# Narrow attentions: a bias row added behind the mix, and fp16 projections in the last attention

## The reference

```
def attention(query, ctx, mask, Wq, bq, Wk, bk, Wv, bv, Wo, bo):   # per batch of 256 tokens
    q = query @ Wq.T + bq;  k = ctx @ Wk.T + bk;  v = ctx @ Wv.T + bv     # 16 heads x 8
    scores = einsum('bhsd,bhtd->bhst', q, k) / sqrt(8)       # layer 1: + bias, mask; layer 3: none
    attn = softmax(scores)
    return einsum('bhst,bhtd->bhsd', attn, v).reshape(B, S, 128) @ Wo.T + bo
x = x + attention(layernorm(x), ctx, ...)
```

## Time and profile before

| | us |
|---|---|
| median of 3 runs | 1505.87 |
| lowest, highest | 1499.92, 1507.51 |
| profiled execution, its own time | 1497.63 |
| span of its instructions | 1495.7 |
| TensorE matmuls busy in it | 1357.8 |
| VectorE, ScalarE, GpSimd busy | 1038.6, 888.9, 820.1 |

### The profile page before, as it was taken

How to read it: one execution, slowest core, us unless ns; L and a number is a source line. 1 busy time by engine, 2 the same in 40 slices (tenths; PEclk the granted TensorE clock), 3 DMA queues, 4 the chain that set the end, 5 groups by cost and what they waited for, 6 DMA issues and landing times.

```text
span 1495.7 us, 37017 instructions
## 1 busy us (share of the span) xinstructions
PE 1357.8 (91%) x14494; PEld 838.4 (56%) x14494; DVE 1038.6 (69%) x2508; ACT 888.9 (59%) x1471; POOL 820.1 (55%) x778
## 2 busy tenths in 40 slices
PE   4799999998979999999978899987978897999988
PEld 3365666665757777777733344433666565444446
DVE  5788888888744344443758989875798476677764
ACT  4487777774759999999834444432233332555542
POOL 6488878776658899989844243212353002434310
PEclk9799999999989999999979999986989899899998
DMA  8000000000013210001101201000000000000000
GB/s 273 5 9 9 9 9 9 2 2 16 30 33 98 61 45 14 28 28 46 33 5 32 65 33 33 30 1 28 1 3 10 0 1 4 5 9 9 2 1 29
DMA packets 25796, 39.62 MB, mean 26 GB/s; under 512 B 7028, under 2 KB 13080, under 8 KB 25144
## 3 DMA queue, kind: packets, MB, share of 16 engines
q1 hardware_dynamic: 25080, 35.58, 7.4%
q0 software_dynamic: 576, 2.10, 0.7%
HBM read 38.72 MB, written 1.05 MB: 27 GB/s over the span
## 4 chain that ended last, share of the span: by engine, by line
PE 67%; DVE 19%; issue 5%; POOL 5%; ACT 3%; DMA 1%; SPq 0%; POOLq 0%; DVEq 0%; ACTq 0%
PE bank L1765 10%; PE bank L1706 10%; PE bank L695 5%; DVE sbuf L834 4%; PE bank L633 4%; PE bank L2231 3%; PE bank L1164 2%; PE bank L649 2%; PE bank L1989 2%; PE bank L1268 2%; POOL sbuf L1118 2%; PE bank L2210 2%; DVE sbuf L851 2%; PE bank L1196 2%; POOL sbuf L1112 2%
## 5 line engine op out<-in xcount | busy, mean ns | idle before, releaser
L1716 ACT ACTIVATE sbuf<-bank,sbuf 128x512 f32<-128x512 f32 (+1 forms) x512 | 323.1, 684 | 30.1 <-PE bank L1706 18.1
L1736 POOL TENSOR_TENSOR sbuf<-sbuf 128x512 f16<-128x512 f32 x256 | 304.9, 1199 | 56.1 <-ACT sbuf L1716 55.1
L310 POOL TENSOR_TENSOR sbuf<-sbuf 128x2 f32<-128x2 f32 (+1 forms) x48 | 39.7, 827 | 353.8 <-DVE sbuf L305 353.8
L1765 PEld LDWEIGHTS bank<-sbuf 128*128 128x128 f16 x3072 | 194.3, 98 | 67.3 <-issue 7.7
L1765 PE MATMUL bank<-sbuf 128*128 128x128 f16 x3072 | 214.6, 220 | 6.3 <-DVEq L1853 6.3
L1706 PE MATMUL bank<-sbuf 128*128 128x512 f16 x768 | 209.2, 382 | 0.0
L834 DVE TENSOR_REDUCE sbuf<-bank 128x4 f32<-128x1024 f32 x128 | 156.3, 1221 | 64.4 <-PE bank L649 51.5
L1848 DVE SCALAR_TENSOR_TENSOR sbuf<-bank,sbuf 128x128 f32<-128x128 f32 x256 | 71.7, 341 | 165.1 <-PE bank L1765 164.9
L1118 POOL TENSOR_TENSOR sbuf<-sbuf 128x512 f16<-128x512 f32 x128 | 148.2, 1179 | 56.8 <-ACT sbuf L1361 56.7
L695 PE MATMUL bank<-sbuf 128*32 128x256 f32 x2048 | 140.3, 393 | 1.6 <-ACT sbuf L782 1.6
L1112 POOL TENSOR_TENSOR sbuf<-sbuf 128x512 f16<-128x512 f32 x96 | 112.0, 1185 | 27.4 <-ACT sbuf L1349 27.1
(11 more groups left out here) (294 smaller groups left out, 2726.8 us busy)
## 6 DMA issues: line engine op xcount, KB each, us to landing
sbuf<-w SPq DMA_DIRECT2D x32, 256.0 KB, 2.9
sbuf<-bias_t SPq DMA_DIRECT2D x4, 1024.0 KB, 11.7
sbuf<-ctx_t SPq DMA_DIRECT2D x24, 128.0 KB, 3.4
sbuf<-bias_q POOLq DMA_DIRECT2D x4, 512.0 KB, 11.6
sbuf<-mask_t SPq DMA_DIRECT2D x8, 256.0 KB, 2.7
sbuf<-bias_t SPq DMA_DIRECT2D x8, 256.0 KB, 3.0
sbuf<-mask_q SPq DMA_DIRECT2D x8, 256.0 KB, 3.7
sbuf<-bias_q SPq DMA_DIRECT2D x8, 256.0 KB, 4.4
```

Source lines behind the costliest of these rows:

```text
L1716: last = act.activation(to, bank[u % 4][:, :], ACT.Gelu, bias=b1[u // U][:, u % FT0:u % FT0 + 1], scale=1 / SCALE)
L1736: g.tensor_tensor(hid16[1][:, u % BUFS, :], hid[:, u % 4, :], hid16[0][:, u % BUFS, :], ALU.subtract)\
L1765: last = pe.matmul(bank[4 + out_no % 2][:, j * P:(j + 1) * P], hid16[h][:, u % BUFS, j * P:(j + 1) * P], w2_16[p][:, w, f * D:(f + 1) * D] ...
```

## The change

It has two parts. In both narrow attentions the bias matmuls of the v and of the output projection go. Once a layer TensorE computes `bv @ Wo.T + bo` (`row` on TensorE, at unit 4), VectorE writes it as three bf16 rows beside a row of ones (`row` on VectorE, at unit 5), and `out` starts each output with three one-row bf16 matmuls over both tiles of 128 tokens, ahead of its wait for the normalised mix. In layer 3 alone the projections of q, k and v become three fp16 passes over halves (high x high, high x low, low x high), with the weights scaled by 256 and ScalarE's scale taking it back. GpSimd makes the halves: of the weights (`weights16`) behind the first `power` of the FFN ahead, of the inputs of batch 0 (`inputs16`) behind the second, and of batch b + 1 behind the splits of batch b.

```diff
-            ("bv1", [D]), ("bo1", [D]),
+            ("bv1", [1]), ("bo1", [D]),
...
+            def weights16(g):
+                at = 0
+                for w, to in zip((wq, wk0, wv), w16):
+                    flat = w if w is wv else w.rearrange("p t c -> p (t c)")
+                    cols = flat.shape[1]
+                    g.tensor_tensor(flat, flat, scale_col[:, 0:1].to_broadcast([P, cols]), ALU.mult)\
+                     .then_inc(s["sixteen"], 1)
+                    g.wait_ge(s["sixteen"], at + 1)
+                    g.tensor_copy(to[:, 0, :], flat).then_inc(s["sixteen"], 1)
+                    g.wait_ge(s["sixteen"], at + 2)
+                    g.tensor_tensor(to[:, 1, :], flat, to[:, 0, :], ALU.subtract).then_inc(s["sixteen"], 1)
+                    at += 3
+
+            def inputs16(g, b):
+                cols = slice(b * S, b * S + S)
+                g.wait_ge(ctx_in[b % 2], b // 2 * 16 + 16)
+                g.wait_ge(nrm_xt, nm.ready(b))
+                wait(g, s["projected"], JOBS * (b - 1))
+                for n, (to, of) in enumerate(((c16[b % 2], ctx_t[b % 2]), (x16[b % 2], xn_t[:, cols]))):
+                    g.tensor_copy(to[:, 0, :], of).then_inc(s["sixteen"], 1)
+                    g.wait_ge(s["sixteen"], WEIGHTS + 4 * b + 2 * n + 1)
+                    g.tensor_tensor(to[:, 1, :], of, to[:, 0, :], ALU.subtract).then_inc(s["sixteen"], 1)
...
                     for k in range(QK):
                         split_(b, k)
+                    if not masked and b + 1 < B:
+                        inputs16(g, b + 1)
...
+                            for n, (w, half16) in enumerate(PASSES):
+                                last = pe.matmul(to[:, c * S:(c + 1) * S], w16[kind][:, w, m * P:(m + 1) * P],
+                                                 (c16 if kind else x16)[b % 2][:, half16, :],
+                                                 start=c == n == 0, stop=c == 1 and n == 2, skip_group_check=True)
...
-                            pe.matmul(o, ct[:, t * P:(t + 1) * P], wv, start=True, stop=False)
-                            last = pe.matmul(o, ones[0:1, :], bv[0:1, :], start=False, stop=True)
+                            if masked:
+                                last = pe.matmul(o, ct[:, t * P:(t + 1) * P], wv, start=True, stop=True)
+                                continue
+                            for n, (w, half16) in enumerate(PASSES):
+                                last = pe.matmul(o, c16[b % 2][:, half16, t * P:(t + 1) * P], w16[2][:, w, :],
+                                                 start=t == n == 0, stop=t == 1 and n == 2, skip_group_check=True)
...
+                def row():
+                    pe.matmul(bank[O_BANK[1]][0:1, 0:D], bv, wo, start=True, stop=False)
+                    pe.matmul(bank[O_BANK[1]][0:1, 0:D], ones[0:1, 0:1], bo[0:1, :], start=False, stop=True)\
+                      .then_inc(s["row"], 1)
...
                 def out(b):
-                    pe.wait_ge(s["normed"], b + 1)
...
+                    if b == 0:
+                        pe.wait_ge(s["row"], 5)
+                    for k in range(3):
+                        pe.matmul(bank[PR][:, 0:S], row16[0:1, 3, :], row16[0:1, k, :].unsqueeze(1).to_broadcast([1, SB, D]),
+                                  start=k == 0, stop=False, skip_group_check=True)
+                    pe.wait_ge(s["normed"], b + 1)
                     for m in range(SB):
-                        o = bank[PR][:, m * P:(m + 1) * P]
-                        pe.matmul(o, att_t[:, m * P:(m + 1) * P], wo, start=True, stop=False)
-                        last = pe.matmul(o, ones[0:1, :], bo[0:1, :], start=False, stop=True)
+                        last = pe.matmul(bank[PR][:, m * P:(m + 1) * P], att_t[:, m * P:(m + 1) * P], wo, start=False,
+                                         stop=m == 1, skip_group_check=True)
...
+                    src, rest = bank[O_BANK[1]][0:1, 0:D], rden[0:1, 0:D]
+                    v.wait_ge(s["row"], 1)
+                    v.tensor_copy(row16[0:1, 0, :], src).then_inc(s["row"], 1)
+                    v.wait_ge(s["row"], 2)
+                    v.tensor_tensor(rest, src, row16[0:1, 0, :], ALU.subtract).then_inc(s["row"], 1)
+                    v.wait_ge(s["row"], 3)
+                    v.tensor_copy(row16[0:1, 1, :], rest).then_inc(s["row"], 1)
+                    v.wait_ge(s["row"], 4)
+                    v.tensor_tensor(row16[0:1, 2, :], rest, row16[0:1, 1, :], ALU.subtract).then_inc(s["row"], 1)
...
                 for k in range(CHUNKS):
                     after.power(g, 2 * k, 2 * k + 2)
+                    if k == 0:
+                        ahead["weights"](g)
+                    if k == 1:
+                        ahead["inputs"](g)
```

More of the change, by code:

```diff
@@ L197, in build @@
             far[name] = take(shape)
+        row_parts = [take([4, D], BF16) for _ in range(2)]
         x_in = [sem(f"x_in{k}") for k in range(CHUNKS)]
@@ L521, in narrow_attention @@
                 "ready",
-            ) if masked or k not in ("masks", "biased")}
+                "row",
+                "sixteen",
+            ) if k not in (("sixteen",) if masked else ("masks", "biased"))}
             ctx_in = [sem(L + f"ctx_in{p}") for p in range(2)]
@@ L540, in narrow_attention @@
             bqs = take([HG])
+            row16 = row_parts[0 if masked else 1]
+            if not masked:
+                w16 = [take([2, HG * P], F16), take([2, HG * P], F16), take([2, D], F16)]
+                x16, c16 = [take([2, S], F16)], [take([2, S], F16)]
+                assert top[0] <= 29888
             if masked:
@@ L559, in narrow_attention @@
             att_t = take([S])
+            if not masked:
+                top[0] = max(top[0], 21040)
+                x16, c16 = x16 + [take([2, S], F16)], c16 + [take([2, S], F16)]
+            SCALE = 1.0 if masked else 2.0 ** 8
+            PASSES = ((0, 0), (0, 1), (1, 0))
+            WEIGHTS = 9
             assert top[0] <= 24832
@@ L632, in project @@
                         for c in range(2):
-                            last = pe.matmul(to[:, c * S:(c + 1) * S], (wq, wk0)[kind][:, 2 * pair + c, :],
-                                             ct if kind else xt, start=True, stop=True)
+                            m = 2 * pair + c
+                            if masked:
+                                last = pe.matmul(to[:, c * S:(c + 1) * S], (wq, wk0)[kind][:, m, :],
+                                                 ct if kind else xt, start=True, stop=True)
+                                continue
[3 more added lines that the diff above has]
+                                                 start=c == n == 0, stop=c == 1 and n == 2, skip_group_check=True)
                     else:
@@ L737, in tensor @@
                         mix(u // 2 - 1, n % 2)
+                    if u == 4:
+                        row()
                     if b + 1 < B and n < JOBS:
@@ L762, in project @@
                             last = act.activation(x32[:, k % 2, c * S:(c + 1) * S], src[:, c * S:(c + 1) * S], ACT.Identity,
-                                                  bias=bias, scale=DH ** -0.5 if kind == 0 else 1.0)
+                                                  bias=bias, scale=(DH ** -0.5 if kind == 0 else 1.0) / SCALE)
                     else:
@@ L910, in narrow_attention @@
             ahead["masks"] = lambda v, k: masks(v, 0, k)
+            ahead["weights"], ahead["inputs"] = weights16, lambda g: inputs16(g, 0)
             programs["sync"].append(sync)
```

21 lines of the change are left out of this document (17 added, 4 removed).

## The result

| | before | after |
|---|---|---|
| median, us | 1504.03 (5 runs) | 1486.71 (5 runs) |
| lowest, highest | 1499.92, 1507.51 | 1480.97, 1491.28 |
| profiled execution, span | 1495.7 | 1484.8 |
| mean granted clock in it | 0.953 | 0.953 |

The ratio is 0.989, with a 95% interval of 0.9862 to 0.9918: 17 us faster where 5 were forecast, and outside the forecast range. The profiled executions differ by less, 10.9 us.

What follows compares the result with a forecast made beforehand. Layer 3's batches were taken as bound by TensorE with equally long waits on VectorE and GpSimd, layer 1's by TensorE and VectorE in turns; the terms summed to -5.0 us, 1505.87 to 1500.9, range 1489 to 1509.

Steps and rivals of the forecast that it cites:

- `out`: Output projection: old price 1.26 us, new 1.27; 0.1 less a batch, bounds 0 and 0.4.
- q and k jobs: Layer 3 projections: 0.76 us for 1.06 each, 1.20 a batch; 0.60 comes through from n=0 and n=1, the rest absorbed.
- v job: Layer 3's v projection: 0.48 us for 1.26, 0.78 less on TensorE, of which 0.08 a batch comes through.
- Starts and ends: Last `out`: -0.8 us in layer 3, -1.2 in layer 1; layer 1's start -1.45, layer 3's -0.3.
- Rows and halves, the added work: Added: `weights16` +1.5 us, `inputs16` +0.3 twice, `row()` +0.8 on TensorE in layer 3, +2.0 on VectorE in layer 1.
- the 0.3 of `inputs16` of batch 1: GpSimd's input halves for batch 1 fall beside layer 3's first cuts: +0.3 us, 0 to 0.7.
- the 0.3 at layer 3's start: Layer 3's first v job: the next turn waits for VectorE's scale, so only some -0.3 us shows.
- layer 1's first 83 us: Start of layer 1: shorter v job -1.45 us, `row()` on VectorE +2.0.
- The second rival: GpSimd's new operations delay VectorE's cut at layer 3's v job 0.4 to 1.1 us a batch: +4.6, 1510.5; chance 0.13.
- The base: Starting time: the difference put on the runs' median, 1505.87 us, not on the profiled execution, 1497.63.
- The first rival: All of TensorE's saving comes through, 14.6 us in place of 5.5: 1490.8, down to 1487; chance 0.22.

Runs made afterwards that it cites:

- alternate: Changed kernel with the one-row passes per tile, three of 128 columns ahead of each output matmul; 1496.24 us, ratio 0.9954 to before.
- out_old: Changed kernel with the output projection in its old form in both layers, combined row kept in f32; 1499.82 us, ratio 0.9985 to before.
- q_only: Changed kernel with fp16 for layer 3's q projections alone, k and v in f32; 1489.38 us, ratio 0.9894 to before.
- v_f32: Changed kernel with layer 3's v projection in f32, q and k in fp16; 1486.08 us, ratio 0.9896 to before.
- rows_only: Changed kernel with layer 3's projections back in f32 and no halves, bias rows kept in both layers; 1490.06 us, ratio 0.9928 to before.
- fp16_only: Changed kernel with fp16 projections in layer 3 kept, both biases by matmul as before; 1496.82 us, ratio 0.9965 to before.
- wait_first: Changed kernel with the wait for the normalised mix ahead of the three one-row passes; 1488.59 us, ratio 0.9902 to before.
- hold: Changed kernel; in layer 3 GpSimd's second half of a k job's split waits until VectorE's cut is done; 1480.2 us, ratio 0.9835 to before.
- hold_early: hold, plus the n=0 second half waiting for VectorE's scale, and weight and input halves ahead of the FFN's powers; 1476.09 us, ratio 0.9832 to before.
- before_hold: Kernel before with the wait of hold alone, projections still f32; 1502.51 us, ratio 0.9995 to before.
- before_again: Kernel before, unedited, profiled once more; 1502.91 us, ratio 1.0007 to before.

## Why the prediction was wrong

The sign of each step and most of the mechanism held; the sum was -5.0 where the runs show -14.0 at one clock. Term by term:

**`out`, "I take 0.1 less, for the sum of the overlaps; the bounds are 0 and 0.4": the step that failed.** It measured 0.49 in layer 3 and in layer 1, outside its bounds. Two readings were wrong. The old price, 1.26, ended at the first record of the work behind, while records of the last bias pair stand after it; from mix to mix it is 1.57, 0.31 more. And the new price, 1.27, took 0.42 for each f32 output matmul from a row where they alternate with one-row matmuls; back to back they cost 0.32, and the whole is 1.07, 0.20 less. alternate and out_old show both. `out` runs seven times in each layer ahead of its last one (six in the periods, once in the last batch), so this is 2 x 7 x 0.39 = 5.5 us of the 9 that are missing.

**q and k jobs.** 0.76 to 0.77 us each, as priced. The 0.60 a batch was right in size and wrong in place: the saving of n = 1 is lost in the wait for VectorE's L330 and that of n = 3 in the wait for the division, those of n = 0 and n = 2 come through. That n = 2's does although the division frees the next scores is due to the cut ahead of it: 0.73 became 0.42, since its split moved along. The prediction said that VectorE's stretch hung on scores issued before those jobs; it also hangs on GpSimd's split, which hangs on the job of n = 1. q_only shows it.

**v job.** 0.44 us (forecast 0.48), absorbed behind the cut: v_f32 leaves the period where it is. From the held scores to the transposes there are 3.02 us (1373.74 to 1376.76) for 3.12: a gain of 0.10, forecast 0.08. The Trainium skill (TensorE: Matmul & The Clock Gate, Back-to-back issue gap) gives 81 ns for a matmul of 128 columns in a stream of weight loads and matmuls. The trace does not quite agree: the six took 0.44 us, 73 ns each, between the page's figure and the 70 that the prediction took from a row.

**Starts and ends.** Layer 1's first v job, from its first matmul to the first scores behind it, takes 3.06 and 3.05 us in the two profiles of the changed kernel, for 4.76 and 4.39 before: 1.5 less (forecast 1.45), part of it work that ran at the higher clock. Both last output projections gained more than forecast. In layer 3 L778 at 1450.19 is followed by the next layer's first matmul 0.66 later; before, that took 1.66 from L710, so 1.0 (forecast 0.8). In layer 1 L778 and the VectorE add behind it (L951) are 0.95 apart in the changed kernel (0.96 in its second profile), for 2.4 before and 3.0 in before's second: 1.4 and 2.0 (forecast 1.2). Much of this is the clock. From that first matmul to the add the granted clock is 1.00 in the changed kernel, and 0.67 and 0.50 before; in all five profiles with the old form it is 0.50 to 0.80, and in eight of the nine with a new form 0.93 or more (rows_only has 0.50, and 1.26 us).
```profile
1003.70 0.50 PE L774 MATMUL bank<-sbuf 1*128 1x256 bf16 x3
1005.63 0.71 PE L778 MATMUL bank<-sbuf 128*128 128x128 f32 x4 [1.43 <-DVE sbuf L946]
```
```profile
1006.58 0.41 DVE L951 TENSOR_TENSOR sbuf<-bank,sbuf 128x256 f32<-128x256 f32 x1
```

**Rows and halves, the added work.** `weights16` stretched four L330 to 3.96 us (forecast 4.2) and its stage by 1.4 (forecast 1.5); `inputs16` of batch 0 stretched the next chunk's four to 2.24 and its stage by 0.25 (forecast 0.3). Together that is 1.65. `row()` on VectorE in layer 1 took 1.94 us from L932 to the next L923 (forecast 2.0), and TensorE waited for it. In layer 3 the same four operations took 1.07, hidden as forecast, and the row's two pairs on TensorE 0.62 (forecast 0.8). No run isolates the 0.3 of `inputs16` of batch 1 and the 0.3 at layer 3's start. Layer 1's row:
```profile
789.29 0.27 DVE L932 CAST sbuf<-bank 1x128 bf16<-1x128 f32 x1
789.59 0.28 DVE L934 TENSOR_TENSOR sbuf<-bank,sbuf 1x128 f32<-1x128 f32 x1
789.91 0.54 DVE L936 CAST sbuf<-sbuf 1x128 bf16<-1x128 f32 x1
790.49 0.81 DVE L938 TENSOR_TENSOR sbuf<-sbuf 1x128 bf16<-1x128 f32 x1
791.23 1.21 DVE L923 TENSOR_TENSOR sbuf<-bank,sbuf 128x1024 f32<-128x1024 f32 x1
```
With the shorter v job counted in, layer 1's first 83 us came out 1.2 us longer, forecast 0.55. In all nine profiles with the four-operation row this stretch has 24 to 31 us at the lower clock, in the five others (among them out_old, which has the shorter v job and one copy for the row) 17 to 21. In four of the nine the first low stretch is longer, ahead of the row, in four a further one stands behind it, and in rows_only both; so the waits behind the shorter v job and behind the row are both suspects, not told apart.

**The second rival** had the right place and the wrong operation. The halves of the inputs, which it feared at the cut, start only as the cut's first half ends (L619 at 1376.26) and stretch its second half from 0.20 to 0.31; it is the split that blocks the first, as splits had before. The Trainium skill (SBUF — State Buffer, Who interferes with whom) says that GpSimd and a VectorE instruction that uses the shared ports exclude each other for a whole instruction and that a tensor_reduce takes no part. The trace agrees: the cut's first half ends within 0.05 us of L635, while L906 at 1368.53, beside another L635, stays at 1.23.

**The base.** The prediction put its difference on the median, which was right: the profiled execution of before was 5 us under the mean of 67 runs. That median, 1505.87 of three runs, was itself 3.5 over this mean.

**The first rival** gave 1490.8 down to 1487 (its own terms give 1488), nearly the measured time, but by luck: not all of TensorE's saving came through, as fp16_only and v_f32 show.

**What stays open.** Layer 3's seven periods are 8.7 and 9.1 us shorter in the two pairs of profiles, its last batch 0.5, layer 1 behind its first 83 us 2.5 and 2.0; with the two ends (-1.0, and -1.7 in the mean), layer 1's first 83 us +1.2 and the weights and inputs +1.65 this is about -11.5, where the runs at one clock show -14.0. The 2 to 3 us between are not placed, and out_old, alternate and wait_first are off from their periods by 1 to 3. The changed kernel's mean clock is higher by 0.0036 (3.4 us), four times the standard error of that difference. Nor is it alone: q_only, v_f32, hold and hold_early have 0.9525 to 0.9532, the kernels with the old output projection (before, before_hold, out_old, fp16_only) 0.9488 to 0.9504. Yet wait_first, which hardly differs from the changed kernel, has 0.9507, and rows_only and alternate 0.9508 and 0.9499. The end of layer 1 accounts for some 0.001 by an estimate (3.0 us at 0.50 gone, of 1500); where the rest arises is not shown.

## What to carry to other kernels

Price a TensorE job from the start of one fixed piece of work to the start of the next of its kind, not from its first record to the first record behind it, and price each new order by rows in that order: f32 matmuls of 128 columns cost 0.32 us each back to back and 0.42 between one-row matmuls. When TensorE's jobs get shorter, look for the stalls that they had covered: the cuts blocked by GpSimd were worth about 1 us before and 5 after, and one wait on GpSimd, which had time, took them away. Before stages of two profiles are compared, compare their granted clock; one stage here differs by 8 us within one kernel.

## What the runs showed of the hardware

Two f32 matmuls of 128 columns with full weights cost 0.65 us back to back (1378.73 to 1379.38) and 0.42 each, 0.84, with one-row matmuls beside them (alternate). Three one-row bf16 matmuls cost 0.42 at 256 columns (1378.31) and 0.27 at 128 (alternate). A VectorE operation on 128x8 elements, 0.18 us alone, lasts to the end of the GpSimd operation that it meets, up to 1.04 us (q_only, 1378.79); two L330 went from 1.30 (changed kernel) to 0.59 once GpSimd's half was held back (hold_early). Layer 1's last output projection in its old form took 2.1 us at a granted clock of 0.80 (before_hold), 2.4 at 0.67 (before) and 3.0 at 0.50 (before_again).
